# Another SBUF layout for the second half: loaded operands 64 bytes behind a multiple of 128, moving operands at a multiple

## The chip, the cores and the metric

The kernel runs on one core of a Trainium2 chip. The metric is the device time of one launch in microseconds (us), the median of the runs; lower is better. Everything is float32 data. Matrix products run on TensorE (PE), which first loads a 128x128 operand (a LDWEIGHTS, shown as PEld; "the loaded operand") and then streams the other one past it (a MATMUL; "the moving operand").

## The reference

For each of 16 samples x (256 tokens of 256 features) with a context of the same shape, four layers run one after the other, each with a residual:

```
x = x + L0_xattn(ctx, layernorm(x))          # 8 heads of 128, keys and values from [ctx, x]: 512 rows
x = x + L0_ffn(layernorm(x))                 # 256 -> 1024 -> 256, gelu; W1 and W2 get a rank-one term per sample
x = x + L1_xattn(layernorm(x), ctx, ctx)     # one head of 256, softmax over 256 context rows
x = x + L1_ffn(layernorm(x))                 # 8 experts: silu(x Wg) * (x Wu), then Wd; weighted by the routing
```

In the last layer all eight experts are computed for every token and summed with the routing weights:

```
gate = einsum('btd,edi->beti', x, Wg); up = einsum('btd,edi->beti', x, Wu)
h = silu(gate) * up
e_out = einsum('beti,eid->betd', h, Wd)
out = einsum('bte,betd->btd', weights, e_out)
```

## The kernel before

**Two halves.** The first half (`latent_attention`, tiles named a_...) runs layer 1 for all 16 samples and keeps the result in HBM. The second half (`ffn_attention_experts`, tiles named b_...) runs layers 2 to 4. Work of sample 0 of the second half lies between the heads of sample 15 of the first (`early`, `spare`, `ahead`, `beside`); from then on one turn t of `rest` runs the experts of sample t-1 and layers 2 and 3 of sample t side by side: 15 such turns (in the trace some 53.5 us each, from 1078 to 1878 us), and a last one of experts alone.

**Products in three parts.** Each float32 operand is held as a high and a low part in fp32r (names ending in h and l), and each product is three matmuls: high x high, high x low, low x high, each with a load of its own. `product` issues them for each of the chunks of the contracted dimension. In the second half a matmul moves 256 columns past a loaded block of 128; in the first half some move 512.

**A turn on TensorE** (written out by hand in `turn` of `tensor`; all engines wait on semaphores of named steps): gate and up of expert 1 (24 matmuls), the four `h_fill` (48; the hidden layer), `down` of expert 0 (12), gate and up 2, `y_fill` (48; the second ffn product), down 1, gate and up 3, `v_fill` (12), the transposes "B" (4), down 2, gate and up 4, `q_fill` (12), down 3, gate 5, `s_fill` (12), up 5, down 4, `t_fill` (4 transposes), gate and up 6, `o_fill` (12), the transposes "A" (4), gate and up 7, down 5, the transposes "C" (4), down 6 and 7, `r_fill` (4), gate and up 0 of the next sample, `r_turned` (2 transposes). This is 432 matmuls of 256 columns by `product`, 4 of `r_fill` and 18 transposes. What is loaded and what moves:

| step | loaded | moving |
|---|---|---|
| gate, up (`into`) | weh, wel | xch, xcl |
| `h_fill` | w1h, w1l | xth, xtl |
| `q_fill` | mh, ml | xth, xtl |
| `s_fill` | hh, hl, chunks 1 and 3 (Q) | cth, ctl |
| `y_fill` | hh, hl | w2h, w2l |
| `o_fill` | hh, hl, chunks 5 and 7 (PT) | hh, hl, chunks 4 and 6 (V) |
| `v_fill` | cth, ctl | wvh, wvl |
| `down` | heh, hel | the third part of weh, wel |
| transposes | ln, pr, rt | ident |

In the profile's names ("ring<-b_xch,b_weh") the moving operand stands first where the loaded one is not ident.

**Addresses.** `Region.put` places each tile by hand: odd=1 puts its start 64 bytes behind a multiple of 128, odd=0 at a multiple, no odd wherever the last one ended. Below, "odd" and "even" stand for these two. `Memory.SIZES` fixes the regions, shared by both halves. hh, hl, w2h and w2l have rows of 272 elements (1088 bytes), so that their chunks alternate between even and odd:

```
w2h, (w2_raw, w2l) = put("low", "w2h", [P, W2ROW * HC], F32R, odd=1), ...   # W2ROW = D + 16
hh, hl = (put("w_values", n, [P, HC, S + 16], F32R, odd=0) ...)
```

So before the change gate, up, `h_fill`, `q_fill`, `s_fill` and `o_fill` load odd and move even (odd/even), `v_fill` and `down` load even and move odd (even/odd), `y_fill` changes between the two with every chunk (3 matmuls), and `r_fill` and all transposes are even/even. In the first half the fills Q, K and O are odd/even, V and the scores even/even, `project_out` is even/odd.

## Time and profile before

| | |
|---|---|
| time, median of 3 runs | 1916.91 us (1916.0 to 1916.91) |
| the profiled execution | 1916.03 us, its span 1914.2 us |
| granted TensorE clock, mean of the span | 0.999 |
| busy: PE, PEld, DVE, ACT, POOL | 98%, 92%, 76%, 64%, 20% |
| chain that ended last | PE 90%, ACT 4%, DVE 4%, issue 2%, DMA 1% |

The span is the time from the first to the last instruction; the profiled time is 1.8 us longer. A matmul's busy time overlaps that of the next, so the share says that PE has work at all times, not that it is at its peak: what the work costs is read from the distance between the starts of two matmuls.

### The profile page before, as it was taken

To read this page: it belongs to the slowest core of one execution; us is meant where nothing else is said; L and a number is where in the kernel's file an instruction comes from. 1 tells how busy PE (TensorE), PEld (TensorE's weight loads), DVE (VectorE), ACT (ScalarE), POOL (GpSimd) and SP (SyncE) were. 2 spreads that over 40 slices of the span, in tenths; PEclk is the share of its full clock that TensorE was granted. 3 is DMA by queue.
4 is the path that set the end of the run, shared out by engine and by line. 5 is a ranking of instruction groups with operands and counts; after the bars stand their busy time and mean duration, and the time that the engine had idled before them with its cause. 6 is when DMAs were issued, how large, how long until landed. Compare 5 with 4: busy or idle time off the path is not lost.

```text
span 1914.2 us, 41511 instructions
## 1 busy us (share of the span) xinstructions
PE 1885.1 (98%) x13822; PEld 1762.0 (92%) x13822; DVE 1463.0 (76%) x3620; ACT 1220.7 (64%) x2554; POOL 387.2 (20%) x610
## 2 busy tenths in 40 slices
PE   7999999999999999999999999999999999999999
PEld 6888888888888888888889899999999999999998
DVE  7877777777777776777667788888888878888776
ACT  5655565556555655565566777667777777767753
POOL 2222122222222222122255201111111111111100
PEclk9999999999999999999999999999999999999999
DMA  3021112111211000000052933423433333433400
GB/s 125 29 72 40 42 60 71 38 44 60 71 37 29 12 22 22 11 11 22 16 105 53 332 78 81 85 58 83 85 72 74 77 71 74 85 74 67 86 7 12
DMA packets 101982, 119.33 MB, mean 62 GB/s; under 512 B 39072, under 2 KB 87072, under 8 KB 101920
## 3 DMA queue, kind: packets, MB, share of 16 engines
q1 hardware_dynamic: 93216, 83.93, 14.5%
q0 software_dynamic: 8704, 34.61, 10.0%
q8 instruction: 35, 0.57, 0.1%
q14 instruction: 27, 0.22, 0.0%
HBM read 97.29 MB, written 21.23 MB: 62 GB/s over the span
## 4 chain that ended last, share of the span: by engine, by line
PE 90%; ACT 4%; DVE 4%; issue 2%; DMA 1%; SPq 0%; POOL 0%; ACTq 0%; DVEq 0%; POOLq 0%
PE ring L649 10%; PE ring L651 10%; PE ring L650 10%; PE ring L1930 9%; PE ring L1932 8%; PE ring L1931 8%; PE ring L702 4%; PE sim L1932 3%; PE sim L1930 3%; PE sim L1931 3%; PE sim L649 3%; PE sim L651 3%; PE sim L650 3%; PE ps_x L649 2%; PE ps_x L650 2%
## 5 line engine op out<-in xcount | busy, mean ns | idle before, releaser
L434 ACT ACTIVATE a_pr<-sim,a_nmax 128x512 f32<-128x512 f32 x256 | 174.2, 688 | 209.1 <-DVE a_nmax L564 209.1
L1930 PE MATMUL ring<-b_xch,b_weh 128*128 128x256 f32 x1024 | 289.7, 283 | 0.5 <-DVE b_act_e L1553 0.5
L1932 PE MATMUL ring<-b_xch,b_wel 128*128 128x256 f32 x1024 | 286.3, 280 | 0.0
L1931 PE MATMUL ring<-b_xcl,b_weh 128*128 128x256 f32 x1024 | 286.0, 279 | 0.0
L345 POOL TENSOR_SCALAR a_pr<-a_pr,a_rinv 128x512 f32<-128x512 f32 x256 | 182.1, 726 | 454.8 <-DVE a_rinv L574 451.9
L1931 PEld LDWEIGHTS ring<-b_xcl,b_weh 128*128 128x128 f32 x1024 | 193.4, 189 | 0.0
L1930 PEld LDWEIGHTS ring<-b_xch,b_weh 128*128 128x128 f32 x1024 | 192.1, 188 | 0.7 <-DVE b_act_e L1553 0.7
L1932 PEld LDWEIGHTS ring<-b_xch,b_wel 128*128 128x128 f32 x1024 | 192.1, 188 | 0.0
L1269 ACT ACTIVATE b_heh<-b_act_e 128x512 fp32r<-128x512 f32 x128 | 80.7, 631 | 146.6 <-DVE b_act_e L1553 112.6
L542 DVE SCALAR_TENSOR_TENSOR a_ktl<-ring,a_bkv_s,a_kth 128x512 fp32r<-128x512 f32 x128 | 95.3, 745 | 98.8 <-ACT a_kth L414 98.7
L555 DVE TENSOR_TENSOR a_ptl<-ring,a_pth 128x512 fp32r<-128x512 f32 x256 | 163.8, 681 | 1.6 <-ACT a_pth L424 0.5
L564 DVE TENSOR_REDUCE a_nmax<-sim 128x1 f32<-128x512 f32 x256 | 163.6, 680 | 0.0
L649 PE MATMUL ring<-a_pth,a_vh 128*128 128x256 f32 x512 | 142.8, 279 | 1.4 <-DVE a_ptl L555 1.3
L551 DVE TENSOR_TENSOR a_vl<-ring,a_vh 128x512 fp32r<-128x512 f32 x128 | 88.4, 691 | 71.8 <-ACT a_vh L422 71.7
L651 PE MATMUL ring<-a_pth,a_vl 128*128 128x256 f32 x512 | 142.6, 279 | 0.0
L650 PE MATMUL ring<-a_ptl,a_vh 128*128 128x256 f32 x512 | 142.5, 278 | 0.0
L422 ACT ACTIVATE a_vh<-ring 128x512 fp32r<-128x512 f32 x128 | 76.6, 599 | 102.1 <-PE ring L651 102.1
L424 ACT ACTIVATE a_pth<-ring 128x512 fp32r<-128x512 f32 x256 | 139.7, 603 | 2.6 <-PE ring L702 2.6
L702 PE MATMUL ring<-ident,a_pr 128*128 128x128 f32 x1024 | 134.1, 273 | 1.9 <-DVE a_ktl L542 1.7
L1553 DVE TENSOR_TENSOR b_act_e<-b_act_e,ring 128x512 f32<-128x512 f32 x128 | 87.6, 684 | 60.2 <-PE ring L1932 46.4
L702 PEld LDWEIGHTS ring<-ident,a_pr 128*128 128x128 f32 x1024 | 118.1, 140 | 16.3 <-DVE a_ktl L542 2.6
L427 ACT ACTIVATE a_oth<-ring,a_bkv_s 128x256 fp32r<-128x256 f32 x128 | 62.1, 485 | 93.0 <-PE ring L651 92.9
(355 smaller groups left out, 6341.3 us busy)
## 6 DMA issues: line engine op xcount, KB each, us to landing
b_w2l_raw<-in_W2T POOLq DMA_DIRECT2D x16, 1088.0 KB, 8.7
b_even_b<-rows_between SPq DMA_DIRECT2D x16, 1024.0 KB, 5.7
b_w1l_raw<-in_W1T POOLq DMA_DIRECT2D x16, 1024.0 KB, 8.4
b_w1l_raw<-in_We SPq DMA_DIRECT2D x8, 768.0 KB, 4.4
expert_halves<-b_w1h SPq DMA_DIRECT2D x8, 768.0 KB, 3.3
expert_halves<-b_w1l SPq DMA_DIRECT2D x8, 768.0 KB, 5.6
b_weh<-expert_halves SPq DMA_DIRECT2D x8, 768.0 KB, 7.5
b_wel<-expert_halves SPq DMA_DIRECT2D x8, 768.0 KB, 8.5
```

The costliest lines, as they stand in the source:

```text
L345: nc.gpsimd.tensor_scalar(pr[:, h % 2, t, :], pr[:, h % 2, t, :], rinv[:, h % 2, t:t + 1], 1.0, ALU.mult, ALU.mult).then_inc(prob_ready, 1)
L424: nc.scalar.activation(pth[:, :, name[2] * P:(name[2] + 1) * P], bank[:].rearrange("p (k q) -> p k q", k=KT), ACT.Copy).then_inc(ring_hi, 1)
L434: nc.scalar.activation(pr[:, h % 2, t, :], sim[t][:], ACT.Exp, bias=nmax[:, h % 2, t:t + 1], accum_out=rsum[:, h % 2, t:t + 1]).then_inc(e ...
L555: nc.vector.tensor_tensor(ptl[:, :, cols], bank[:].rearrange("p (k q) -> p k q", k=KT), f32(pth[:, :, cols]), ALU.subtract).then_inc(ring_ ...
L564: nc.vector.tensor_reduce(nmax[:, h % 2, t:t + 1], sim[t][:], AX.X, ALU.max, negate=True)\
L649: nc.tensor.matmul(out, lh, rh, start=(n == 0), stop=False)
L650: nc.tensor.matmul(out, lh, rl, start=False, stop=False)
L651: last = nc.tensor.matmul(out, ll, rh, start=False, stop=(n == len(parts) - 1))
L702: last = nc.tensor.transpose(bank[:, k * P:(k + 1) * P], pr[:, h % 2, t, k * P:(k + 1) * P], ident[:])
L1930: nc.tensor.matmul(out, lh, rh, start=(n == 0), stop=False)
L1931: nc.tensor.matmul(out, lh, rl, start=False, stop=False)
L1932: last = nc.tensor.matmul(out, ll, rh, start=False, stop=(n == len(parts) - 1))
```

## The change

All of it is in where the second half's tiles lie.

- w2h and w2l start even and lose their padding (rows of 1024 bytes); the eight memsets of GpSimd that zeroed the padding go.
- hh and hl become one block of rows of 1024 bytes that starts odd; V gets a view of its own that starts 16 elements further (even), over what were chunks 6 and 7; Q is chunks 1 and 3, PT chunks 4 and 5.
- The down part of each expert's weights lies 16 elements behind gate and up, so gate and up stay odd and down is even. Each half of an expert is loaded by two DMAs instead of one, 32 instead of 16 in all, once in the kernel.
- heh, hel, ln, pr and wr start odd.
- The regions change size, so that most tiles of both halves move by a multiple of 128 bytes.

cth, ctl, wvh and wvl keep their places, so `v_fill` stays even/odd; rt stays even. No matmul is added, removed or put elsewhere.

```
-    SIZES = (("low", 50688), ("small", 1664), ("inputs", 14 * KB), ("w_values", 17 * KB), ("w_queries", 16 * KB + 128),
-             ("values0", 16 * KB + 128), ("w_keys", 24 * KB + 128), ("scores", 24 * KB + 128),
-             ("values1", 48 * KB + 128), ("probs", 8 * KB), ("rows", 4 * KB))
+    SIZES = (("low", 49536), ("small", 1664), ("inputs", 14 * KB + 256), ("w_values", 16 * KB + 256), ("w_queries", 16 * KB + 128),
+             ("values0", 16 * KB + 128), ("w_keys", 24 * KB + 512), ("scores", 24 * KB + 512),
+             ("values1", 49 * KB), ("probs", 8 * KB + 64), ("rows", 4 * KB))
...
-W2ROW = D + 16
+W2ROW = D
...
-    w2h, (w2_raw, w2l) = put("low", "w2h", [P, W2ROW * HC], F32R, odd=1), put(
-        "low", "w2l", [P, W2ROW * HC], F32R, raw=True, odd=1)
+    w2h, (w2_raw, w2l) = put("low", "w2h", [P, W2ROW * HC], F32R, odd=0), put(
+        "low", "w2l", [P, W2ROW * HC], F32R, raw=True, odd=0)
...
-    x1_s, ln = put("inputs", "x1_s", [P, ST, D]), put("inputs", "ln", [P, ST, D])
+    x1_s, ln = put("inputs", "x1_s", [P, ST, D]), put("inputs", "ln", [P, ST, D], odd=1)
...
-    pr = put("inputs", "pr", [P, ST, S])
+    pr = put("inputs", "pr", [P, ST, S], odd=1)
...
-    HROW = S + 16
-    hh, hl = (put("w_values", n, [P, HC, HROW], F32R, odd=0) for n in ("hh", "hl"))
-    Q, V, PT = (slice(n, n + 3, 2) for n in (1, 4, 5))
+    hid = [put("w_values", n, [P, HC * S + 16], F32R, odd=1) for n in ("hh", "hl")]
+    hh, hl = (t[:, 0:HC * S].rearrange("p (c s) -> p c s", c=HC) for t in hid)
+    vvh, vvl = (t[:, (HC - 2) * S + 16:].rearrange("p (c s) -> p c s", c=ST) for t in hid)
+    Q, PT = slice(1, 4, 2), slice(4, 6)
...
-    wr = put("w_queries", "wr", [P, DC, P], F32R)
+    wr = put("w_queries", "wr", [P, DC, P], F32R, odd=1)
...
-    heh, hel = (put("probs", n, [P, 2, 2, S], F32R, odd=0) for n in ("heh", "hel"))
+    heh, hel = (put("probs", n, [P, 2, 2, S], F32R, odd=1) for n in ("heh", "hel"))
...
-        weh.append(put(HOME[e], f"weh{e}", [P, 3, DC, D], F32R, odd=1))
-        raw, low = put(HOME[e], f"wel{e}", [P, 3, DC, D], F32R, raw=True, odd=1)
-        we_raw.append(raw)
-        wel.append(low)
+        for what, halves_of in (("weh", weh), ("wel", wel)):
+            halves_of.append(put(HOME[e], f"{what}{e}", [P, 3 * DC * D + 16], F32R, odd=1))
+
+    def gate_up(tile):
+
+        return tile[:, 0:GU].rearrange("p (j c d) -> p j c d", j=2, c=DC)
+
+    def down_of(tile):
+
+        return tile[:, GU + 16:].rearrange("p (c d) -> p c d", c=DC)
...
-                sp.dma_start(f32(tile[:]).rearrange("p j c d -> p (j c d)"), kept[part, e]).then_inc(expert_in[e], 16)
+                sp.dma_start(f32(tile[:, 0:GU]), kept[part, e][:, 0:GU]).then_inc(expert_in[e], 16)
+                sp.dma_start(f32(tile[:, GU + 16:]), kept[part, e][:, GU:]).then_inc(expert_in[e], 16)
...
-                for c in range(HC):
-                    last = nc.gpsimd.memset(f32(w2_raw[:, c * W2ROW + D:(c + 1) * W2ROW]), 0.0)
...
-                last = product(cd[:, k, :], range(ST), lambda c: hh[:, PT.start + 2 * c, q], lambda c: hl[:, PT.start + 2 * c, q],
-                               lambda c: hh[:, V.start + 2 * c, 0:S], lambda c: hl[:, V.start + 2 * c, 0:S])
+                last = product(cd[:, k, :], range(ST), lambda c: hh[:, PT.start + c, q], lambda c: hl[:, PT.start + c, q],
+                               lambda c: vvh[:, c, :], lambda c: vvl[:, c, :])
...
-                               lambda c: hel[:, e % 2, c, q], lambda c: weh[e][:, 2, c, :],
-                               lambda c: wel[e][:, 2, c, :])
+                               lambda c: hel[:, e % 2, c, q], lambda c: down_of(weh[e])[:, c, :],
+                               lambda c: down_of(wel[e])[:, c, :])
...
-                pe.wait_ge(expert_in[0], 32)
+                pe.wait_ge(expert_in[0], 64)
```

## Rows read from the trace of the kernel before

**Rows 1.** The page: the span, busy time by engine, the last chain by engine.

```profile
span 1914.2 us, 41511 instructions
PE 1885.1 (98%) x13822; PEld 1762.0 (92%) x13822; DVE 1463.0 (76%) x3620; ACT 1220.7 (64%) x2554; POOL 387.2 (20%) x610
...
PE 90%; ACT 4%; DVE 4%; issue 2%; DMA 1%; SPq 0%; POOL 0%; ACTq 0%; DVEq 0%; POOLq 0%
```

**Rows 2.** Busy time by stage: first half, then turns of the second half.

```profile
30.00:850.00 820.00, 815.01 (x5214) 723.88 (x5214) 614.92 (x1360) 491.81 (x1117) 198.64 (x314) 1.00 0.12 39
...
1010.00:1860.00 850.00, 844.96 (x7105) 835.12 (x7104) 684.67 (x1882) 600.97 (x1173) 128.92 (x198) 1.00 0.38 87
```

**Rows 3.** Timeline of PE (start, duration, what): first matmul of gate 0, successive turns.

```profile
1447.57 0.28 PE L1930 MATMUL ring<-b_xch,b_weh 128*128 128x256 f32 x1
...
1501.15 0.28 PE L1930 MATMUL ring<-b_xch,b_weh 128*128 128x256 f32 x1
```

**Rows 4.** The same timeline: gate 3 to `v_fill`; then up 5, down 4, `t_fill`.

```profile
1470.28 0.28 PE L1930 MATMUL ring<-b_xch,b_weh 128*128 128x256 f32 x1
...
1473.10 0.29 PE L1930 MATMUL ps_c<-b_wvh,b_cth 128*128 128x256 f32 x1
...
1484.76 0.28 PE L1930 MATMUL ring<-b_xch,b_weh 128*128 128x256 f32 x1
...
1486.12 0.28 PE L1930 MATMUL ring<-b_weh,b_heh 128*128 128x256 f32 x1
...
1487.54 0.60 PE L2005 MATMUL sim<-ident,b_pr 128*128 128x128 f32 x4
```

**Rows 5.** The same timeline: down 0, which follows `h_fill`, to gate 2.

```profile
1459.10 0.28 PE L1930 MATMUL ring<-b_weh,b_heh 128*128 128x256 f32 x1
...
1460.47 0.28 PE L1930 MATMUL ring<-b_xch,b_weh 128*128 128x256 f32 x1
```

**Rows 6.** The same timeline: the transposes "B", down 2, gate 4.

```profile
1474.48 0.60 PE L1941 MATMUL sim<-ident,b_ln 128*128 128x128 f32 x4
1474.84 0.36 PE L1930 MATMUL ring<-b_weh,b_heh 128*128 128x256 f32 x1
1475.04 0.28 PE L1931 MATMUL ring<-b_wel,b_heh 128*128 128x256 f32 x1
...
1476.34 0.28 PE L1930 MATMUL ring<-b_xch,b_weh 128*128 128x256 f32 x1
```

**Rows 7.** The same timeline, first half: fill Q after transposes; another, then fill O.

```profile
507.32 0.28 PE L650 MATMUL ring<-a_kvl,a_wqh 128*128 128x256 f32 x1
...
508.62 0.28 PE L649 MATMUL ring<-a_pth,a_vh 128*128 128x256 f32 x1
...
519.37 0.28 PE L649 MATMUL ring<-a_kvh,a_wqh 128*128 128x256 f32 x1
...
520.73 0.28 PE L649 MATMUL ring<-a_pth,a_vh 128*128 128x256 f32 x1
...
522.09 0.39 PE L649 MATMUL ring<-a_wvh,a_kvh 128*128 128x512 f32 x1
```

**Rows 8.** The same timeline: `q_fill` to down 3; `o_fill` to the transposes "A".

```profile
1479.16 0.28 PE L1930 MATMUL sim<-b_xth,b_mh 128*128 128x256 f32 x1
...
1480.53 0.28 PE L1930 MATMUL ps_x<-b_weh,b_heh 128*128 128x256 f32 x1
...
1490.80 0.28 PE L1930 MATMUL sim<-b_hh 128*128 128x256 f32 x1
...
1492.23 0.60 PE L1941 MATMUL ps_c<-ident,b_ln 128*128 128x128 f32 x4
```

**Rows 9.** Waits of PEld in 1010 to 1860 us: total, times, longest.

```profile
PEld ring L1941 <- DVE b_ln L1504: 4.1, 14, 0.3
PEld ring L1930 <- DVE b_hel L1557: 2.5, 14, 0.2
```

**Rows 10.** Timeline of SP's queue: the last load of an expert.

```profile
1090.96 0.43 SPq L1009 DMA_DIRECT2D b_wel<-expert_halves  x1
```

**Rows 11.** Instructions on b_hh: one group of `o_fill`: durations min/median/max, first and last start.

```profile
L1930 PE MATMUL sim<-b_hh x60: 279/280/283, 1116.0 to 1866.7; 128*128 128x256 f32 x60
```

More of the change, by code:

```diff
@@ L868, in ffn_attention_experts @@
     top_f = put("values0", "top_f", [P, ST, 2])
-    heh, hel = (put("probs", n, [P, 2, 2, S], F32R, odd=0) for n in ("heh", "hel"))
+    heh, hel = (put("probs", n, [P, 2, 2, S], F32R, odd=1) for n in ("heh", "hel"))
     HOME = ["w_keys"] * 2 + ["scores"] * 2 + ["values1"] * 4
-    weh, we_raw, wel = [], [], []
+    GU = 2 * DC * D
+    weh, wel = [], []
     for e in range(E):
-        weh.append(put(HOME[e], f"weh{e}", [P, 3, DC, D], F32R, odd=1))
-        raw, low = put(HOME[e], f"wel{e}", [P, 3, DC, D], F32R, raw=True, odd=1)
-        we_raw.append(raw)
-        wel.append(low)
+        for what, halves_of in (("weh", weh), ("wel", wel)):
[4 more added lines that the diff above has]
+        return tile[:, GU + 16:].rearrange("p (c d) -> p c d", c=DC)
     a_ring, a_sim, ps_c, ps_x = first.banks
@@ L1138, in early @@
                 for e in range(E):
-                    nc.gpsimd.memset(index[:, e:e + 1], float(e))
-                for c in range(HC):
-                    last = nc.gpsimd.memset(f32(w2_raw[:, c * W2ROW + D:(c + 1) * W2ROW]), 0.0)
+                    last = nc.gpsimd.memset(index[:, e:e + 1], float(e))
                 last.then_inc(consts, 1)
@@ L1369, in beside @@
             if (h, done) == (5, "begin"):
-                copy_high(0, "V", hh[:, V, 0:S])
+                copy_high(0, "V", vvh)
                 act.wait_ge(uv_step, 2)
@@ L1420, in turn @@
                 if chain:
-                    copy_high(t, "V", hh[:, V, 0:S])
+                    copy_high(t, "V", vvh)
                 if more:
@@ L1784, in beside @@
             if (h, done) == (5, "maxima"):
-                copy_low(0, "V", hl[:, V, 0:S], hh[:, V, 0:S])
+                copy_low(0, "V", vvl, vvh)
                 queries_low(0)
@@ L1860, in turn @@
                 if chain:
-                    copy_low(t, "V", hl[:, V, 0:S], hh[:, V, 0:S])
+                    copy_low(t, "V", vvl, vvh)
                 weigh(i, 2)
@@ L2035, in into @@
                 cols = slice(k * P, (k + 1) * P)
-                last = product(ps[:, k * S:(k + 1) * S], range(DC), lambda c: weh[e][:, w, c, cols],
-                               lambda c: wel[e][:, w, c, cols], lambda c: xch[:, c, :], lambda c: xcl[:, c, :])
+                last = product(ps[:, k * S:(k + 1) * S], range(DC), lambda c: gate_up(weh[e])[:, w, c, cols],
+                               lambda c: gate_up(wel[e])[:, w, c, cols], lambda c: xch[:, c, :], lambda c: xcl[:, c, :])
             return last
@@ L2143, in turn @@
                 i = t - 1
-                pe.wait_ge(expert_in[1], 32)
+                pe.wait_ge(expert_in[1], 64)
                 gate(i, 1)
@@ L2155, in turn @@
                 down(i, 0)
-                pe.wait_ge(expert_in[2], 32)
+                pe.wait_ge(expert_in[2], 64)
                 gate(i, 2)
@@ L2166, in turn @@
                 down(i, 1)
-                pe.wait_ge(expert_in[3], 32)
+                pe.wait_ge(expert_in[3], 64)
                 gate(i, 3)
@@ L2176, in turn @@
                 down(i, 2)
-                pe.wait_ge(expert_in[4], 32)
+                pe.wait_ge(expert_in[4], 64)
                 gate(i, 4)
@@ L2184, in turn @@
                 down(i, 3)
-                pe.wait_ge(expert_in[5], 32)
+                pe.wait_ge(expert_in[5], 64)
                 gate(i, 5)
@@ L2194, in turn @@
                     t_fill(t)
-                pe.wait_ge(expert_in[6], 32)
+                pe.wait_ge(expert_in[6], 64)
                 gate(i, 6)
@@ L2203, in turn @@
                     transposed(t + 1, "A")
-                pe.wait_ge(expert_in[7], 32)
+                pe.wait_ge(expert_in[7], 64)
                 gate(i, 7)
```

## The prediction, made before the changed kernel ran

> **What bounds the kernel now.** I read the page first: PE has work 98% of a span of 1914.2 us, and 90% of the chain that ended last is PE [rows 1]. The table by stage says the same of the turns of the second half: in 850 us PE is busy 844.96 us, VectorE 684.67 (81%), ScalarE 600.97 (71%), at a granted clock of 1.00 throughout [rows 2]. The waits in those turns are small: the longest total, before the transposes "C", is 4.1 us, the next 2.5 us [rows 9]. So the time is the number of matmuls times the distance between their starts, which I call the pace, and the timeline of PE is the view that shows it. There the reader is to see that one and the same matmul has two paces. Gate and up 3 are 24 matmuls in 1473.10 - 1470.28 = 2.82 us, 117.5 ns each; up 5 is 12 in 1486.12 - 1484.76 = 1.36 us, 113.3 ns each [rows 4]. The clock is the same, nobody waits, the operands are equally odd/even in both. Whichever pace a step has, it keeps to its end: the fast one is 113.3 ns, the slow one 117.5 to 118.
>
> How much is at stake: a turn, from gate 0 to gate 0, takes 1501.15 - 1447.57 = 53.58 us [rows 3]. In it lie 436 matmuls of 256 columns and 18 transposes. A group of four transposes costs 1475.04 - 1474.48 = 0.56 us with the slow restart behind it, one matmul of which (0.12) belongs to the 436 [rows 6], so about 0.44; three such groups, the "C" group with its waits (I allow 0.9, an estimate) and the pair of `r_turned` (half, 0.22) make 2.4 us. The rest, 51.1 us over 436, is 117.3 ns: nearly everything is slow. All at 113.3 would save 436 x 4.0 = 1.7 us a turn, and over the 16 samples' worth of such work 27 us. All at 117.7 would cost 436 x 0.4 = 0.2 us a turn, 3 us in all. This asymmetry carries the forecast.
>
> **What sets the pace.** I followed the pace over all turns at each border between steps.
> - Fast, and the direction flips: slow afterwards. Up 5 is fast, down 4 behind it takes (1487.54 - 1486.12)/12 = 118 ns [rows 4]; gate 2 after the fast down 0 is slow again. That held in all 16 turns for down 4.
> - Fast, and the direction stays: fast. In the first half a fast fill Q (1.36 us for 12, 113.3) is followed by a fast fill O (1.36 us, 113.3) [rows 7]; so up 5 after `s_fill`.
> - Slow, and the direction flips: often fast. Down 0 behind the slow `h_fill` takes 1.37/12 = 114 ns [rows 5].
> - Slow, and the direction stays: mostly slow, but it can fall to fast. `q_fill` behind a slow up 4 takes 1.37/12 = 114 ns here [rows 8], in 9 of 15 turns; `s_fill` ends fast in all 15; `h_fill` never does; a fill O in 2 of 22. Together 26 of 67, about 0.4 per border.
> - After transposes: slow. Down 2 takes (1476.34 - 1475.04)/11 = 118 ns [rows 6], and so do gates 1, 6 and 7; in the first half a fill Q behind transposes has (508.62 - 507.32)/11 = 118 [rows 7].
>
> Fast thus lasts while the direction is constant, and a flip destroys it; the change makes it constant except in `v_fill`.
>
> **The change part by part.**
> - Flips removed (heh/hel odd, down part even, hh/hl odd, w2 even): in the five stretches between transposes the pace can now only fall from slow to fast. I take that each stretch starts slow and that at every border 0.6 of the slow ones remain. Matmuls at the slow pace: behind `r_turned` 24 + 29 + 4 + 5 + 6 + 1 + 1 = 70, and 12 of `v_fill`, which still flips; behind "B" 12 + 14 + 4 + 3 + 2 + 1 = 36; behind `t_fill` 24 + 7 = 31; behind "A" 24 + 7 = 31; behind "C" 24 of down 6 and 7, 2 of `r_fill` and 9 of gate and up 0, 35. The sum is 215 of 436. At 4.2 ns each that is 0.9 us a turn above the fast floor, where before it is about 1.7 less rounding (1.6): a gain of 0.7 us a turn, over 15 turns 10.5 us. Bounds: nothing leaks, and also down 0, down 1 and the fast parts of `y_fill` are lost, +3 us; everything is fast at once, -27 us.
> - ln and pr odd: the transposes become odd/even as their neighbours. Nothing in the trace shows an odd transpose. Its own pace hardly can fall; what matters is in which pace the next step starts. From below: as now, 0. From above: fast, which with the point before gives the full -27. I take 0, since restarts are slow behind even transposes whether odd/even or even/odd follows [rows 6, 7].
> - Rows of 1024 bytes: `o_fill`, whose chunks alternate in the bit of 128 bytes, takes 1.43/12 = 119 ns [rows 8], the slowest of all. With equal rows it should take 113 to 118: -12 x 1 to 6 ns a turn, at most 1 us in all; I count it as within the sum.
> - The two halves of an expert now lie 6272 bytes apart, a multiple of 128 but not of 256, where before they lay 6144 apart. This brings the alternation of `o_fill` into gate and up. As `s_fill`, which has it in the loaded operand alone, ends fast, I take 0; the other end is a rival below.
> - 16 more DMAs on SP's queue: the last load of an expert occupies the queue 0.43 us [rows 10], so 16 x 0.43 = 7 us of SP over 45 us of the seam, and behind them the loads of first rows, context and x1 for the next turn start up to 3 us later. Expert 7 is issued at 1090.96 and used behind the first `o_fill`, which starts at 1116.0 [rows 10, 11]: 25 us of cover. Nothing; without cover up to 3 us, once.
> - Memsets of GpSimd gone, 20% busy [rows 1]: nothing. VectorE and ScalarE read and write the same number of elements; they stand at 81% and 71% in the turns, so a turn 1.7 us shorter (3%) still leaves them room: nothing, though the wait at "C" may grow by some of it.
> - The first half keeps its parities; only multiples of 128 move: nothing, with 2 us to either side.
>
> The sum is made against the profiled 1916.0 us: 1916.0 - 10.5 = 1905.5. The median is 0.9 above that execution, so 1906 us.
>
> The Trainium skill, "TensorE: Matmul & The Clock Gate", in the part "Step-by-step: what each phase is for", speaks against the change: TensorE reads the moving operand and the weights through two independent ports, and loading the next weights takes no bandwidth from the running matmul. By that rule addresses do not matter, and the sum would be 0. The trace bears it out only in part: a matmul of the same shape at the same clock goes at 113.3 or at 118 ns [rows 4], and something in how the two streams meet must tell the two apart.
>
> **The rivals.**
> - *Fast from the restart on.* Odd transposes leave TensorE in the fast pace, and nothing but `v_fill` disturbs it. For it: the fast pace never ended without a flip or a restart. Against it: 118 behind every group of transposes [rows 6, 7]. Time: 1916.9 - 27, plus what `v_fill` and the wait at "C" keep, 1892 us.
> - *The slow pace stays.* The direction is not what matters; steps start slow behind transposes and remain so, as `h_fill` always does, and the flips were what made down 0 and down 1 fast [rows 5]. Time: +3, and what leaks at `q_fill` and `s_fill` back, 1917 to 1920 us. This is also the case that the change does nothing.
> - *Slower: the alternation of 128 bytes spreads.* Gate and up load, and down moves, high and low parts that differ in that bit, and they take the 119 ns of `o_fill` [rows 8] instead of the slow pace's 117.5. For it: `o_fill` and `y_fill`, which mix the bit in both operands, are never steadily fast. Against it: `s_fill`. The price is 288 of 436 matmuls x 1.5 ns plus the 0.2 us of lost fast steps, 0.65 us a turn: 10 us, so 1927. It decides if the pace of gate and up passes 118.5.
>
> **How the numbers follow.** Chances: the forecast (partly fast) 0.40, fast from the restart 0.17, the slow pace stays 0.28, slower 0.15. A change of 0.2%, 3.8 us, is about what a measurement of this kernel can tell from none. The first two cases are faster, 0.57; the third lies within 3.8 us, 0.28; the last is slower, 0.15. The range reaches from the all-fast case to the slow one, 1892 to 1920 us; outside are most of the last case and a gain beyond the second. The forecast's own range is 1898 to 1913.
>
> **What the profile after would show.** If I am right, gate and up of later experts in a stretch stand at 113.3 ns in the timeline, down 3 and 4 too, a turn takes some 52.9 us, and the steps behind transposes still start at 118. The step most likely wrong is the 0.4 per border. Fast gates 1, 6 and 7 would show the second case (a turn of 51.9 us), gates at 118 throughout the third, above 118.5 the last. A wait of PE for an expert, or a longer one before "C", would show that the DMAs or VectorE were not hidden.

## The result, and the profile after

The changed kernel takes 1923.69 us (median of 7 runs, 1922.45 to 1926.16), the one before 1916.91 beside it (7 runs): 1.0035 times as long, 95% interval 1.0026 to 1.0045. It is slower by 6.8 us; forecast was 1906, 11 us less. The profiled execution took 1922.45 us. Its page, in the lines that answer to [rows 1]:

```profile
span 1920.6 us, 41519 instructions
...
PE 1892.1 (99%) x13822; PEld 1768.7 (92%) x13822; DVE 1461.0 (76%) x3620; ACT 1221.4 (64%) x2554; POOL 387.4 (20%) x602
...
PE 89%; DVE 4%; ACT 4%; issue 2%; DMA 1%; POOL 0%; SPq 0%; ACTq 0%; DVEq 0%; POOLq 0%
```

```profile
1010.00:1860.00 850.00, 844.60 (x7082) 834.50 (x7081) 680.75 (x1877) 601.55 (x1174) 131.87 (x201) 1.00 0.38 86
```

The second fence is the table by stage, as in [rows 2] (stretch, busy time and count of PE, PEld, DVE, ACT and POOL, then the granted clock). PE was as busy and the clock as high as in [rows 2], but it got through 7082 matmuls in the stretch instead of 7105. The waits are those of [rows 9] too:

```profile
PEld ring L1948 <- DVE b_ln L1511: 4.0, 14, 0.3
PEld ring L1937 <- DVE b_hel L1564: 2.5, 14, 0.2
```

So the loss is pace, not waiting. The timeline of PE shows where. First the first half, the same fill Q, fill O and next product as in [rows 7]:

```profile
521.16 0.28 PE L649 MATMUL ring<-a_kvh,a_wqh 128*128 128x256 f32 x1
...
522.52 0.28 PE L649 MATMUL ring<-a_pth,a_vh 128*128 128x256 f32 x1
...
523.94 0.40 PE L649 MATMUL ring<-a_wvh,a_kvh 128*128 128x512 f32 x1
```

Fill Q is fast (1.36 us, 113.3 ns each), fill O behind it slow (1.42 us, 118.0), where [rows 7] has 1.36. The instructions on `a_pth` (durations min/median/max; first the kernel before, then the changed one) say that this is general: the median of 512 matmuls goes from 276 to 280 ns. A matmul's own duration is a usable mark of the pace: 276 or 277 where it is fast, 279 or 280 where it is slow.

```profile
L649 PE MATMUL ring<-a_pth,a_vh x512: 276/276/415, 36.2 to 1066.9; 128*128 128x256 f32 x171
```

```profile
L649 PE MATMUL ring<-a_pth,a_vh x512: 275/280/357, 36.4 to 1069.5; 128*128 128x256 f32 x171
```

Then a turn of the second half, from gate 0 to gate 0, with gate 3 in its first seven matmuls:

```profile
1451.54 0.28 PE L1937 MATMUL ring<-b_xch,b_weh 128*128 128x256 f32 x1
...
1474.52 0.28 PE L1937 MATMUL ring<-b_xch,b_weh 128*128 128x256 f32 x1
1474.64 0.28 PE L1938 MATMUL ring<-b_xcl,b_weh 128*128 128x256 f32 x1
1474.76 0.28 PE L1939 MATMUL ring<-b_xch,b_wel 128*128 128x256 f32 x1
1474.88 0.28 PE L1937 MATMUL ring<-b_xch,b_weh 128*128 128x256 f32 x1
1474.99 0.28 PE L1938 MATMUL ring<-b_xcl,b_weh 128*128 128x256 f32 x1
1475.12 0.28 PE L1939 MATMUL ring<-b_xch,b_wel 128*128 128x256 f32 x1
1475.24 0.28 PE L1937 MATMUL ring<-b_xch,b_weh 128*128 128x256 f32 x1
...
1477.38 0.28 PE L1937 MATMUL ps_c<-b_wvh,b_cth 128*128 128x256 f32 x1
...
1481.98 0.28 PE L1937 MATMUL ring<-b_xch,b_weh 128*128 128x256 f32 x1
...
1483.34 0.28 PE L1937 MATMUL sim<-b_xth,b_mh 128*128 128x256 f32 x1
...
1484.70 0.28 PE L1937 MATMUL ps_x<-b_weh,b_heh 128*128 128x256 f32 x1
...
1486.11 0.28 PE L1937 MATMUL ring<-b_xch,b_weh 128*128 128x256 f32 x1
...
1505.34 0.28 PE L1937 MATMUL ring<-b_xch,b_weh 128*128 128x256 f32 x1
```

The turn takes 53.80 us, against 53.58 in [rows 3]. Gate and up 3 take 2.86 us for 24, 119.2 ns each, where [rows 4] has 117.5: one distance in six is long (1474.99 to 1475.12; 124 ns in the unrounded starts), which the kernel before hardly has. Up 4 and `q_fill` are fast (1.36 us each), but down 3 behind them is not (1.41), although nothing flips any more.

I summed the distances from each matmul's start to the next over the trace, by step (us). Below, a step is called fast where its inner distances are about 113.3 ns. All such sums and counts are of the one profiled execution of each kernel; the kernel before and e8, which differ by 256 bytes alone, are up to 0.8 us apart in single steps and 2.1 in the first half as a whole, so smaller differences say little.

| | before | after |
|---|---|---|
| first half, without its transposes | 905.5 | 909.8 |
| of it fill O | 178.7 | 183.0 |
| gate and up | 365.0 | 366.3 |
| `down` | 186.4 | 187.6 |
| `h_fill` | 91.7 | 91.7 |
| `y_fill` | 90.0 | 91.2 |
| transposes of both halves | 163.1 | 162.2 |
| of them first half | 133.2 | 132.2 |

Fill O alone loses 4.3 us. With its transposes, which gain 1.0, the first half loses 3.3 us, about half of the 6.4 us between the two profiled executions, and the change touches nothing of its code. In the second half gate and up have 437 distances of 124 ns instead of 21, yet a larger fast share (0.22 instead of 0.14); `down` has lost its fast steps. "Behind a down" below counts the gates that directly follow a `down` (gates 2 to 5 of the turns and a few at the ends), 65 in all: 1 is fast before, 15 after.

### The profile page after: what moved, and what is told of

It is laid out like the page before. It is cut to its first block, busy times and chain, and to the rows that moved or that the text cites. A ratio compares the mean times of both kernels' runs of the same rounds, so it can differ in the third digit from the quotient of the medians.

```text
span 1920.6 us, 41519 instructions
## 1 busy us (share of the span) xinstructions
PE 1892.1 (99%) x13822; PEld 1768.7 (92%) x13822; DVE 1461.0 (76%) x3620; ACT 1221.4 (64%) x2554; POOL 387.4 (20%) x602
## 4 chain that ended last, share of the span: by engine, by line
PE 89%; DVE 4%; ACT 4%; issue 2%; DMA 1%; POOL 0%; SPq 0%; ACTq 0%; DVEq 0%; POOLq 0%
PE ring L649 10%; PE ring L651 10%; PE ring L650 10%; PE ring L1937 9%; PE ring L1938 8%; PE ring L1939 8%; PE ring L702 4%; PE sim L1938 3%; PE sim L1937 3%; PE sim L1939 3%; PE sim L649 3%; PE sim L651 3%; PE sim L650 3%; PE ps_x L649 2%; PE ps_x L650 2%
## 5 line engine op out<-in xcount | busy, mean ns | idle before, releaser
L702 PEld LDWEIGHTS ring<-ident,a_pr 128*128 128x128 f32 x1024 | 118.0, 140 | 15.4 <-DVE a_ktl L542 2.3
```

Of the source, the lines that this page charges most:

```text
L702: last = nc.tensor.transpose(bank[:, k * P:(k + 1) * P], pr[:, h % 2, t, k * P:(k + 1) * P], ident[:])
```

## The experiments

All times are medians, ratios are to the kernel before on the same chip. The theories that the expectations name by letter are said in them; in my words they are three: *places* (the pace of a step depends on where its two operands start within 256 bytes, and an operand that alternates by 128 bytes costs), *direction* (the prediction's: a flip between odd/even and even/odd ends the fast pace), and *dealt anew* (the pace at a step's start depends on what ran before, so any move of anything shuffles it). Places within 256 bytes, where they matter: a_pth 128 in both kernels, a_kvh 128 before and 0 after; xth 0, w1h 192 in both; xch 128 before, 0 after; after, weh 192 and wel 64, hh 192 and hl 64, heh and hel 192.

**e1, the first half's move alone, on the kernel before.** Everything between `low` and `values1` moves 128 bytes down; `a_pth` stays.

```
-    SIZES = (("low", 50688), ...  ("values1", 48 * KB + 128),
+    SIZES = (("low", 50560), ...  ("values1", 48 * KB + 256),
```

> The kernel before, with every region except the first (low) and the last two (probs, rows) 128 bytes lower; odd and even stay as they are everywhere. The tiles of attention weights (pth, ptl) and heh, hel now stand otherwise to the rest in the bit of 128 bytes, as they do in the changed kernel. Theory A (most of the loss is not from odd and even but from this bit: the fills O of the first half start fast only if their moving operand continues in the bit of 128 bytes where that of the fill before left off): fills O go from 115 to about 117.7 ns, 1536 of them, +4 us, so 1921 us. Rival B (a move by 128 bytes does nothing, the loss comes from the direction being constant in the second half): within 1 us of the kernel before.

1917.11 us, 1.0003 (0.9994 to 1.0012). The first half without its transposes went from 905.5 to 910.0, fill O from 178.7 to 183.0 us, as in the changed kernel:

```profile
L649 PE MATMUL ring<-a_pth,a_vh x512: 276/280/356, 36.2 to 1069.2; 128*128 128x256 f32 x171
```

The total missed its expectation of 1921. The first half's transposes gained 1.5 us and gate and up 1.0 (364.0), and the profiled execution, 1918.27 us, is 1.2 us above the median, so fill O's loss is in the trace and hardly in the time. That loss comes from places and from no other part of the change: the edit moves the regions between `low` and `probs` by 128 bytes against `a_pth`. Fill O's own pairs stay the same two (loaded 64 or 192, moving 128; the two halves of the heads change over). What differs is the moving operand against that of the fill before it. The traces of all 16 kernels that do the whole work say the same: where a_kvh and a_pth have one place (eight kernels), every one of 245 fast fills Q is followed by a fast fill O; where they are 128 bytes apart (the other eight), none of 215 is.

**e2, the same move undone, on the changed kernel.**

```
-    SIZES = (("low", 49536), ...  ("values1", 49 * KB),
+    SIZES = (("low", 49408), ...  ("values1", 49 * KB + 128),
```

> The changed kernel, with all regions between low and probs 128 bytes lower, so that the first half has its old relation of pth to the keys' and values' tiles in the bit of 128 bytes. Theory A: the fills O are fast again, -4 us against the changed kernel, about 1919 to 1920 us. Rival B: the time stays at 1923 to 1924 us.

1907.43 us, 0.9953 (0.9939 to 0.9966): 16 us less than the changed kernel and faster than both. Fill O is back at 179.3 us; the rest came where I had expected nothing: `h_fill` 88.5, `y_fill` 87.5, gate and up 362.0, 49 of 65 gates fast behind a down. The timeline of a turn (up 1, `h_fill`, down 0, gate 2, up 2, `y_fill`, down 1; the turn ends at 1496.02 and began at 1443.13, 52.9 us):

```profile
1447.57 0.28 PE L1937 MATMUL ring<-b_xch,b_weh 128*128 128x256 f32 x1
...
1448.93 0.28 PE L1937 MATMUL sim<-b_xth,b_w1h 128*128 128x256 f32 x1
...
1454.37 0.28 PE L1937 MATMUL ring<-b_weh,b_heh 128*128 128x256 f32 x1
...
1455.77 0.28 PE L1937 MATMUL ring<-b_xch,b_weh 128*128 128x256 f32 x1
...
1458.50 0.28 PE L1937 MATMUL sim<-b_w2h,b_hh 128*128 128x256 f32 x1
...
1463.96 0.28 PE L1937 MATMUL ps_x<-b_weh,b_heh 128*128 128x256 f32 x1
```

`h_fill` takes 5.44 us for 48, 113.3 ns, a pace that it has in neither kernel; down 0 behind it is slow (1.40), in the same direction. Its moving operand alternates.

**e3, high and low part of an expert a multiple of 256 bytes apart,** on the changed kernel. For experts 0 and 1 the order weh0, weh1, wel0, wel1 does it, for the others a gap:

```
+    for e in range(2, E):
+        placed["weh", e] = put(HOME[e], f"weh{e}", [P, 3 * DC * D + 16], F32R, odd=1)
+        of[HOME[e]].top += 128
+        placed["wel", e] = put(HOME[e], f"wel{e}", [P, 3 * DC * D + 16], F32R, odd=1)
```

> The changed kernel, with the high and the low part of each expert a multiple of 256 bytes apart (in the changed kernel 6272 bytes, which is not one); the first half as in the changed kernel. Theory A2 (in a slow step a matmul whose loaded operand changes in the bit of 128 bytes costs 6.7 ns more, once in six): the matmuls of 124 ns vanish from gate and up, about 3072 x 0.75 x 1.1 ns = 2.5 us less than the changed kernel, 1921 us. Rival (these are noise of the steps' mixture): no change.

1913.1 us, 0.9988 (0.9979 to 0.9997), 10.6 us less than the changed kernel. The distances of 124 ns fall from 437 to 16, gate and up from 366.3 to 361.2, `down` to 186.1, and, unexpected, `h_fill` and `y_fill` to 88.7 and 87.5; fill O stays slow (182.7). Only part of the 10.6 us is the alternation itself: 421 long distances fewer, each with its five neighbours 6 x (118.9 - 117.8) = 6.6 ns, make some 2.8 us, an estimate. The rest are steps that start fast, as `h_fill`, of which no operand moved. The edit also moves one half of each expert by 128 bytes, and e9, which removes the alternation too, gains far less.

**e4, the paces by themselves.** A kernel of TensorE work alone that leaves out all of the reference's work (its output is a copy of x): blocks of 36 matmuls of 128x256 behind four transposes, for all 16 pairs of places; a, b, c, d are 0, 64, 128, 192 bytes in 256. Then alternating operands, then pairs of blocks of 24 without transposes between them.

```
+    last = nc.tensor.matmul(ps[:, 0:256], ld[la if k == 2 else a][:, 0:128],
+                            mv[lb if k == 1 else b][:, 0:256], start=True, stop=True)
```

> TensorE alone, none of the kernel's work (the output is a copy of the input x): blocks of 36 matmuls of 128x128 by 128x256 in fp32r, each behind four transposes, for each of 16 pairs of positions (a, b, c, d: 0, 64, 128, 192 bytes behind a multiple of 256) of the loaded and the moving operand, behind even and behind odd transposes and behind a wait; then with one of the operands alternating by 128 bytes, and then 24 matmuls at one pair of positions followed by 24 at another. Theory A: two paces, 113.3 and about 117.7 ns, decided by the positions of the step and of what ran before it, and a step keeps its pace. Rival C (the slow pace is contention with the other engines or the DMAs, which stand still here): all blocks at one pace.

Its timeline merges a block into one row (start, duration, moving and loaded operand). Of a row of 36 the last matmul takes 0.28 us and the first distance is 0.20; the other 34 distances give the pace.

```profile
51.76 4.52 PE L76 MATMUL ps_m<-mv_d,ld_b 128*128 128x256 f32 x36
...
74.98 4.49 PE L76 MATMUL ps_m<-mv_a,ld_d 128*128 128x256 f32 x36
...
84.38 4.36 PE L76 MATMUL ps_m<-mv_c,ld_d 128*128 128x256 f32 x36
...
88.92 4.56 PE L76 MATMUL ps_m<-mv_d,ld_d 128*128 128x256 f32 x36
...
248.62 2.98 PE L76 MATMUL ps_m<-mv_a,ld_b 128*128 128x256 f32 x24
251.44 2.99 PE L82 MATMUL ps_n<-mv_c,ld_b 128*128 128x256 f32 x24
...
254.63 3.07 PE L76 MATMUL ps_m<-mv_a,ld_b 128*128 128x256 f32 x24
...
538.70 2.98 PE L76 MATMUL ps_m<-mv_b,ld_c 128*128 128x256 f32 x24
541.52 2.89 PE L82 MATMUL ps_n<-mv_c,ld_b 128*128 128x256 f32 x24
```

Every other engine idles here, and the paces are there: from (4.56 - 0.48)/34 = 120.0 ns for both operands at the same place, 118.4 to 118.8 for other pairs of equal parity, to 113.3 or 117.8 for odd/even and even/odd. In this first pass behind even transposes seven of the eight odd/even and even/odd pairs are fast, all but d loaded with a moving (4.49); behind odd transposes four are, behind a wait none. But this is one draw each, and the pairs of blocks show that neither the pair of places nor the transposes decide a start: the block of b loaded with a moving, behind the same even transposes, is fast at 248.62 (2.98 us) and slow at 254.63 (3.07), and of the 128 first blocks, eight times each of eight pairs behind even and behind odd transposes, 52 are fast. Only one of the 16 cases is the same all eight times. A loaded operand that alternates by 128 bytes gives 113.3, or 118.9 with one 124 in six; a moving one that alternates gives 117.8 in all eight blocks, never 113.3.

The rows from 248.62 on speak of the border between two blocks. Written as loaded/moving: from b/a to b/c, same direction, moving operand 128 bytes on, fast turns slow ((2.99 - 0.28)/23 = 117.8); from c/b to b/c, a flip, fast stays fast ((2.89 - 0.28)/23 = 113.5). Of the 52 fast blocks of 24 the next stays fast in 7 of 7 where the moving operand stays in its place, in 8 of 17 where it goes on by 64 bytes, and in none of 28 where it moves by 128 or back by 64. Fill O in the kernel before is of the first kind (a_kvh and a_pth both at 128), in the changed one of the last.

The same count can be made in the turns of the second half of the 16 kernels, for borders from a fast step to a step of another kind, with the places taken from the kernels' addresses (without `o_fill`, `r_fill` and the padded `y_fill`). The border keeps the fast pace in 617 of 618 cases where the moving operand's place stays and does not alternate, in 26 of 115 where it goes on by 64 bytes, in none of 241 where it goes back by 64, in 45 of 212 where it moves by 128 (all 45 into a `y_fill` whose loaded operand alternates), and in none of 283 where the next moving operand alternates. A flip of direction is always a move by 64 one way or the other, and 26 of these 356 cases keep the pace; so the rule of the prediction was a part of this one.

**e5, e6, e7, e8: all together, hh/hl alone, down alone, and a control.** e5 is e2 and e3, with hl a multiple of 256 bytes behind hh. e6 is the changed kernel with that last edit alone. e7 puts the low down parts of experts 2 to 7 128 bytes further, gate and up unmoved. e8 is the kernel before with every region between `low` and `values1` moved 256 bytes.

```
+    hid = []                                    # e5, e6
+    for n in ("hh", "hl"):
+        hid.append(put("w_values", n, [P, HC * S + 16], F32R, odd=1))
+        of["w_values"].top += 128
...
+    gap = [16 if e < 2 else 48 for e in range(E)]          # e7
+    wel.append(put(HOME[e], f"wel{e}", [P, 3 * DC * D + gap[e]], F32R, odd=1))
...
-    SIZES = (("low", 50688), ...  ("values1", 48 * KB + 128),      # e8
+    SIZES = (("low", 50432), ...  ("values1", 48 * KB + 384),
```

> The changed kernel with everything brought together: high and low parts of every expert, and of hh and hl, a multiple of 256 bytes apart, and the first half's relation of pth to the keys' tiles as before (as in the second experiment). Theory D (an operand that alternates by 128 bytes between its high and low part costs; a moving one keeps a step from ever being fast, a loaded one adds 6.7 ns to every sixth matmul of a slow step; where a step starts is set by its position against that of the step before): no matmul of 124 ns in gate and up, and down has fast steps; 1907.4 us of the second experiment less 2 to 8, 1900 to 1906 us. Rival E (the start of a step is so sensitive that each layout deals the paces anew, whatever the alternation): anywhere from 1895 to 1918 us, and the pace of down as before.

> The changed kernel with hh and hl a multiple of 256 bytes apart (8448, in the changed kernel 8320), and the other regions where they were in the bit of 128 bytes. Theory D: the 124 ns matmuls vanish from y_fill (its pace 118.55 falls to 117.7, or to 113 if it now starts fast), down 1 behind it may change; 0.7 to 4 us less than the changed kernel, 1920 to 1923 us. Rival E: a change of up to 5 us either way with the pace of other steps moving as much as y_fill's.

> The changed kernel with the down parts of the high and low halves of experts 2 to 7 at the same place in the bit of 128 bytes (gate and up stay alternating, experts 0 and 1 as in the changed kernel). Theory D: down of experts 2 to 7 can be fast, in some of them its pace falls from 118 to 113.3; down in all from 117.66 ns to 115 to 117 ns, 1 to 4 us less, 1920 to 1923 us. If down stays above 117.5 in all experts, the alternation of the moving operand is not what keeps it slow.

> The kernel before with all regions between low and probs 256 bytes lower: no tile changes in the bits of 64 and 128 bytes. Theory D: nothing changes, 0.9995 to 1.0005, and the pace of each step is as before. Rival E (any move deals the paces anew): the first half's fills or the second half's steps change pace.

- e8: 1916.94 us, 1.0000 (0.9991 to 1.0009). 256 bytes change nothing in the time, so only the place within 256 counts there. In its trace single steps still start otherwise (`q_fill` fast in 14 of 15 turns against 9, down 6 in 13 against 4).
- e7: 1920.75 us, 1.0027 (1.0017 to 1.0036). `down` falls from 187.6 to 186.5, down 4 is fast in 15 turns and down 6 in 13. As expected.
- e6: 1923.12 us, 1.0035 (1.0021 to 1.0049). In `y_fill` the 119 distances of 124 ns go (91.2 to 90.6 us); gate and up take it back (367.1). A wash.
- e5: 1910.97 us, 0.9974 (0.9963 to 0.9985), against 1900 to 1906 expected. Gate and up (361.3) and `down` (185.9) are as good as in e3, but `h_fill` (91.1) and `y_fill` (90.4) are slow. Gains of single edits don't add: the steps' starts were dealt anew, which was the rival of its expectation.

**e9, the experts' layout of before, on the changed kernel.** No gap, heh and hel even, down flips the direction again, halves a multiple of 256 bytes apart.

```
-            halves_of.append(put(HOME[e], f"{what}{e}", [P, 3 * DC * D + 16], F32R, odd=1))
+            halves_of.append(put(HOME[e], f"{what}{e}", [P, 3 * DC * D], F32R, odd=1))
...
-    heh, hel = (put("probs", n, [P, 2, 2, S], F32R, odd=1) for n in ("heh", "hel"))
+    heh, hel = (put("probs", n, [P, 2, 2, S], F32R, odd=0) for n in ("heh", "hel"))
```

> The changed kernel with one part undone: the experts' weights lie as before the change (no gap, down loads even and moves odd, heh and hel even, high and low parts a multiple of 256 bytes apart), all else as changed. Theory D (what counts is which positions within 256 bytes the two operands have and that neither alternates by 128; the direction odd/even or even/odd by itself keeps nothing): the 437 matmuls of 124 ns in gate and up go to under 30, gate and up take 361 to 364 us of 366.3, some down steps become fast (185.5 to 186.5 us of 187.6), fill O of the first half stays slow (183), and the kernel comes to 1914 to 1918, near that in which only the expert halves were set a multiple of 256 bytes apart (1913.1) although all eight down steps flip the direction again. Theory of the prediction (a flip destroys the fast pace): no gate behind a down is fast, down 4 behind a fast up 5 slow; gate and up 365 or more, 1919 to 1922. Theory E (fast starts are dealt anew by anything): anything between, with other steps (q_fill, s_fill, h_fill) moving by up to 4 us in either direction.

1922.33 us, 1.0029 (1.0019 to 1.0039): not the 1914 to 1918 of *places*, but what *direction* gave. The alternation is gone (20 distances of 124 ns), yet gate and up only fall to 364.5 us and `down` stays at 187.2. Of 65 gates behind a down 12 are fast. But all halves lie at 192 here and at 64 or 192 in e3, so the run doesn't part the two; e15 does.

**e10, e11, e12: three edits on e2.** e10 adds the gap of e7, e11 the placing of e3, e12 puts ln and pr back at even places, with all matmul operands of `product` unmoved.

```
-    pr = put("inputs", "pr", [P, ST, S], odd=1)           # e12, and the same for ln
+    pr = put("inputs", "pr", [P, ST, S], odd=0)
...
+    of["inputs"].top += 128                               # behind ln, so that xth stays
```

> The fastest version so far (the changed kernel with the regions between low and values1 moved back by 128 bytes, 1907.4) and in it the down parts of experts 2 to 7 a multiple of 256 bytes apart, as was done alone on the changed kernel (1920.75 of 1923.7, down 187.6 to 186.5). Theory D: down 4 and 6 become fast, down 186 to 186.7 us, the rest as in the fastest version: 1905.5 to 1907. Theory E: down gains the same, but h_fill, y_fill or gate and up lose what they had (in that version 88.5, 87.5 and 362.0), 1907 to 1914.

> The fastest version so far (1907.4) and in it high and low part of each expert a multiple of 256 bytes apart, as was done alone on the changed kernel (1913.1). Nothing is done to hh and hl, which are still 8320 bytes apart. Theory D, sums of the single effects: first half 906.5, gate and up 361, down 186, h_fill 88.6, y_fill 87.5 (118 ns only if it starts slow): 1903 to 1906. Theory E: like the version with all three (1910.97), in which h_fill and y_fill had become slow: 1908 to 1912. If y_fill is fast here, it was the moving of hl by 128 bytes that made it slow there.

> The fastest version so far (1907.4) with ln and pr at even places as before the change, every other tile of weight unmoved (x2_s moves by 64 bytes). Tells what odd transposes alone are worth. Theory F (odd transposes let a step start fast, as gate 6 did in 15 of 15 turns behind those of pr): gate 6, up 6 and o_fill become slow, at 24 to 36 matmuls x 4.4 ns x 15 turns 1.6 to 2.4 us, and what starts behind ln too where it is fast; 1909 to 1912. Theory D alone (the place of loaded and moving operand of the step itself decides): no change, 1906.5 to 1908.5. The transposes' own pace may move by under 1 us.

- e10: 1905.51 us, 0.9942 (0.9930 to 0.9955), the fastest seen; its interval overlaps that of e2. `down` 186.0 as expected, gate and up 359.8.
- e11: 1907.44 us, 0.9947 (0.9931 to 0.9963), runs from 1901.3 to 1911.0, a wide spread for one layout, of which the trace shows one execution (1907.4). `down` 185.1, `y_fill` 87.4, but `h_fill` back at 91.4, slow behind slow up 1 in 14 turns. Within 256 bytes the tiles of e5 and e11 differ in hl alone, and `y_fill` is fast here: hl's move made it slow in e5, as far as one trace of each can tell.
- e12: 1907.76 us, 0.9957 (0.9944 to 0.9970), as e2. Gates behind transposes: 40 of 45 fast against 20; gates behind a down 34 of 65 against 49; `q_fill` slow (22.6 against 21.9). Moving the transposes' operand shuffles the starts and is worth nothing in sum.

**e13, e14: the two relations that e2 moved, each alone.** e13 moves `probs` (a_pth, heh, hel) by 128 against all else, e14 `low` (w1, w2).

```
-    SIZES = (("low", 49536), ...  ("values1", 49 * KB),
+    SIZES = (("low", 49280), ...  ("values1", 50304),         # e13
+    SIZES = (("low", 49408), ...  ("values1", 49 * KB),       # e14
```

> The changed kernel with only probs (a_pth, a_ptl of the first half; heh, hel of the second) moved by 128 bytes against all else (other regions move by 256, which did nothing in the control). Theory D: fill O goes back to 179.3 us of 183.0, first half 906.3; down's operand relation changes, its sum 187.6 stays or becomes fast in part; h_fill, y_fill and gate and up as in the changed kernel (91.7, 91.2, 366): 1919.5 to 1920.5 of 1923.7. Rival: h_fill and y_fill became fast in the version with both moves because the downs beside them ran differently; then they fall here too and the time comes to 1908 to 1912.

> The changed kernel with only low (w1h, w1l, w2h, w2l) moved by 128 bytes against all else, probs included. Theory D: fill O stays slow (183, first half 910), h_fill falls to 88.5 and y_fill to 87.5 us from 91.7 and 91.2, and what follows them (gate and up) to about 362: 1911 to 1913. Rival: the relation of heh and hel to the down parts is what let the gates behind down start fast; then gate and up stay at 366 and the time is 1916 to 1919.

1914.6 us, 0.9991 (0.9982 to 1.0) and 1914.58 us, 0.9994 (0.9984 to 1.0003). The instructions of `h_fill`, `y_fill` and fill O, first e13, then e14:

```profile
L1937 PE MATMUL sim<-b_xth,b_w1h x120: 278/280/357, 1065.5 to 1829.0; 128*128 128x256 f32 x120
...
L1939 PE MATMUL sim<-b_w2h,b_hl x240: 276/276/280, 1091.0 to 1841.6; 128*128 128x256 f32 x120
...
L649 PE MATMUL ring<-a_pth,a_vh x512: 276/279/357, 36.8 to 1069.3; 128*128 128x256 f32 x171
```

```profile
L1937 PE MATMUL sim<-b_xth,b_w1h x120: 276/276/356, 1066.1 to 1828.6; 128*128 128x256 f32 x120
...
L1939 PE MATMUL sim<-b_w2h,b_hl x240: 276/276/283, 1091.6 to 1841.3; 128*128 128x256 f32 x120
...
L649 PE MATMUL ring<-a_pth,a_vh x512: 276/280/357, 36.3 to 1069.8; 128*128 128x256 f32 x171
```

Both missed their expectations (1919.5 to 1920.5 and 1911 to 1913). `h_fill` is fast in e14 (88.5 us) and slow in e13 (91.7), as *places* had it from the place of w1 against xth, 192 and 128 or 192 and 0. Over all kernels that does not hold: at 192 and 128 it is slow in e1 (91.7) and e11, at 192 and 0 fast in e3 (88.7) and e15 (88.9). Behind a fast up 1, as in nearly every turn of e14, e3 and e15, `h_fill` is fast (80 of 80 in the 16 kernels, the moving place being the same); behind a slow one it starts fast in e2 and slow in e13 and e1, and that stays open. `y_fill` is fast in both, in e13 though neither of its operands moved against the other: there 63 of 65 gates behind a down became fast, up 2 among them, and `y_fill` goes on from it. That is the rival of e13's expectation, in part. Fill O fell only to 181.1 in e13, with fill Q up by 1.2, because there was less to carry: only 3 of the 61 fills Q in front of a fill O are fast there, against 35 in e2, and all 3 keep their pace. Why fill Q starts slow in e13 stays open. In time the two add up: 1.0035 - 0.9991 and 1.0035 - 0.9994 make 0.0085, e2 has 0.0082.

**e15, down's direction alone.** e3, with heh and hel even and the down part 64 bytes earlier, so that it is odd; every operand of gate and up stays in its place. This is the prediction's "flip" put back by itself.

```
-        return tile[:, GU + 16:].rearrange("p (c d) -> p c d", c=DC)
+        return tile[:, GU:GU + DC * D].rearrange("p (c d) -> p c d", c=DC)
...
-    heh, hel = (put("probs", n, [P, 2, 2, S], F32R, odd=1) for n in ("heh", "hel"))
+    heh, hel = (put("probs", n, [P, 2, 2, S], F32R, odd=0) for n in ("heh", "hel"))
```

> The version in which only the expert halves were set a multiple of 256 bytes apart (1913.1) and in it down's direction turned back (heh and hel even, the down part 64 bytes earlier so that it is odd); every operand of gate and up stays exactly in its place. Direction theory (a flip at each border of down takes the fast pace away, as the prediction said): gates behind a slow down, of which 17 of 33 were fast, become slow, gate and up rise from 361.2 to 364 or more, h_fill and y_fill (88.7, 87.5) to 91, and the time is 1919 to 1923. Theory D alone (position pair of the step itself, not the direction before it): gate and up stay within 1 us of 361.2, only down moves (186.1 by up to 1.5 us), 1912 to 1915.

1911.89 us, 0.9981 (0.9972 to 0.9990), e3 0.9988: not slower. Gate and up 360.8 us (361.2 in e3), 28 of 65 gates fast behind a down (32), `down` 185.6 (186.1). `y_fill` is slow (91.2 against 87.5 in e3) and `q_fill` and `s_fill` fast instead. Putting the flips back costs nothing that can be measured in sum; a constant direction is not what the loss or a gain hangs on.

## Why the prediction was wrong

It failed at the step "Fast thus lasts while the direction is constant, and a flip destroys it", from which the -10.5 us came, and at two terms set to nothing. In place of the direction the runs showed that fast lasts while the moving operand keeps its place within 256 bytes and does not alternate (7 of 7 borders in e4, 617 of 618 in the turns of the second half, 245 of 245 from fill Q to fill O).

- *Two paces with no wait between them:* right. They are 113.3 and 117.8 ns, and e4 has them with all other engines idle. The Trainium skill ("TensorE: Matmul & The Clock Gate", "Step-by-step: what each phase is for") says that loading the next weights takes no bandwidth from the running matmul; by that the time would not have moved at all, and e2, e3, e13 and e14 move it by addresses alone, by 9 to 16 us.
- *"Fast, and the direction flips: slow"; "fast, and the direction stays: fast":* I had read a rule of parity out of borders at which the place within 256 bytes changed too. The changed kernel breaks it in the first half (fast fill Q, slow fill O) and at `q_fill` to down 3; e4 breaks it both ways in its own blocks; e15 puts the flips back and nothing is lost. In the borders that I read, flip and change of place went together; parity was the coarse half of a finer quantity.
- *The 0.4 per border,* and with it the 215 slow matmuls of a turn: a mean over borders of different kinds, with no meaning for a new layout. Of the gates in the changed kernel 4 and 6 are fast in all 15 turns, the others in at most one.
- *The first half, "nothing, with 2 us to either side":* +4.3 us in fill O, +3.3 in all. It keeps its parities, as I said, but a_kvh moved by 128 and a_pth did not. e1 shows the cost on the kernel before (fill O 178.7 to 183.0), e2 takes it back. I had looked at places within 128 bytes only.
- *The halves 6272 bytes apart, "I take 0":* here `s_fill`, which ends fast with an alternating loaded operand, misled me; e4 says that such a step is either 113.3 or 118.9, by its start. Gate and up got 437 distances of 124 ns; e3 takes them away. And `down`, whose moving operand alternates, lost its fast steps (186.4 to 187.6) and ends the fast pace: of 17 fast steps in front of a down none goes on, although the down's high part lies at the same place. This kept the second half from the gain that I forecast as much as anything; e7 makes downs 4 and 6 fast again.
- *Odd transposes 0:* right in sum (e12), though gate 6 behind those of pr is fast in 15 of 15 turns, where I had all restarts slow. That is not the odd place: in e12, with pr even, it is fast in 15 too, in e2, with pr odd, in none.
- *o_fill at most 1 us:* right, 23.2 to 22.9 us. *DMAs, memsets, VectorE, ScalarE nothing:* right; the waits of [rows 9] are unchanged and the last load of an expert is issued at 1095.45, 23 us ahead of the first `o_fill` at 1118.4.

Of the rivals the third, slower by the alternation, came nearest: 1927 against 1923.7, in part by luck. Its mark did not show (gate and up stand at 117.7 ns on average, below the 118.5 at which it was to decide), because their fast share rose while the slow ones went to 118.9; and about half of the loss is not its mechanism but the first half's. Shown are the first half's cause (e1, e2), what the alternation does to gate, up and `down` (e3, e4, e7; not that it is all of e3's gain, see e9) and that direction is none (e15). When a step loses the fast pace the bench foretells for the whole kernel. When a slow step falls into the fast pace stays open, so the time of a layout can't be forecast: the bench's first blocks do it in 52 of 128 cases, not fixed by their places. Not tested is the layout that the count asks for, all moving operands of the second half at one place and none alternating.

## What to carry to other kernels

Where TensorE is bound by its pace, read it from start to start in the timeline for each step, and note operands' places within 256 bytes, not 128, for loaded and moving operand and for the step before, in every half of the program that shares the memory map, edited or not. Let successive steps have their moving operands at the same place within 256 bytes, and keep the high and low parts of one operand a multiple of 256 bytes apart, the moving one above all; then try the few shifts of whole regions by 128 bytes, each of which costs a line: they were worth 16 us against the changed kernel here, more than the whole redesign. Don't add up gains of single moves, and part a rule read off correlated borders (parity) from its finer cousin (place) before a layout is built on it.

## What the runs showed of the hardware

- The same fp32r matmul of 128x256 with a load of its own has a start-to-start distance of 120.0 ns where both operands lie at the same place within 256 bytes, of 118.4 to 118.8 where they lie 128 apart, and of 113.3 or 117.8 where they lie 64 or 192 apart, at a granted clock of 1.0 (e4). Which of the last two is not fixed by the places: the same block behind the same transposes shows both (52 of 128 fast).
- A fast step stays fast behind a border at which the moving operand keeps its place, and loses the pace where it moves by 128 or back by 64 (7 of 7 and 0 of 28 in e4; 617 of 618 and, where neither operand alternates, 0 of 407 in the second halves of 16 kernels).
- A shift of regions by 128 bytes moves the time by up to 16 us, one by 256 bytes by nothing (e2 against e8).
- An operand that alternates by 128 bytes: loaded, 113.3 or 118.9 ns with one distance of 124 in six; moving, 117.8 and never fast (e4).
- Two regions (`low` and `probs`) shifted by 128 bytes against the rest, with no instruction changed, are worth 0.8% of this kernel (e2 against the changed kernel).
